# A decoder layer with a state-space mixer on one core: the first block's opening reordered, and the second block's softplus spread over more places

## The reference, cut to what matters

```python
x = x + mixer(layernorm(x))                      # x: 32 sequences of 64 tokens, 512 wide
x = x + attention(layernorm(x), ctx, ctx, mask)
x = x + lora_experts(layernorm(x))

def mixer(h):                                    # 128 heads of 64, 8 groups, state 128
    gate, xBC, dt = split(h @ in_proj_w.T)
    xBC = silu(conv4(xBC) + conv_b)              # causal, 4 taps
    hs, B, C = split(xBC)
    dt = softplus(dt + dt_bias)
    cum = cumsum(dt * -exp(A_log))               # along the tokens
    y = (C @ B.T * exp(cum_i - cum_j) * dt) @ hs + D * hs    # causal
    g = y * silu(gate)
    return rms_norm_by_group(g) * norm_w @ out_w.T
```

## Time and profile before

| | |
|---|---|
| median of 3 runs | 2931.94 us |
| the profiled execution, its own time | 2934.74 us |
| its span | 2932.8 us |
| TensorE busy | 97% of the span |
| VectorE, ScalarE, GpSimd busy | 69%, 50%, 44% |
| mean granted TensorE clock | 0.983 |
| chain that ended last | TensorE 86%, VectorE 8%, ScalarE 3% |

### The profile page before, as it was taken

The page is one execution under the profiler, slowest core; times in us unless marked ns, Lnnn a source line. Parts: engine busy times, 40 slices in busy tenths (PEclk is TensorE's granted clock), DMA queues, the critical chain, the costliest instruction groups (busy, mean ns, idle before and its releaser), DMA issues.

```text
span 2932.8 us, 56348 instructions
## 1 busy us (share of the span) xinstructions
PE 2842.4 (97%) x22240; PEld 2295.3 (78%) x22240; DVE 2022.1 (69%) x3160; ACT 1453.3 (50%) x2184; POOL 1305.0 (44%) x834
## 2 busy tenths in 40 slices
PE   4999999999999999999999999999999999999997
PEld 3777787777878888887888878888888888888875
DVE  6677777777666766677666676677666666666657
ACT  3655665555453555544444544554545454454433
POOL 3576666566443334434334433334334334343423
PEclk8999999999999999999999999999999999999996
DMA  6778777777655655656656655555655555565520
GB/s 190 263 265 280 272 260 255 249 262 237 218 187 184 194 171 185 194 173 187 203 182 197 195 170 184 182 182 186 200 182 187 192 188 185 181 196 177 180 94 19
DMA packets 179267, 578.26 MB, mean 197 GB/s; under 512 B 25216, under 2 KB 31872, under 8 KB 170816
## 3 DMA queue, kind: packets, MB, share of 16 engines
q1 hardware_dynamic: 179008, 574.66, 59.7%
HBM read 460.29 MB, written 114.29 MB: 196 GB/s over the span
## 4 chain that ended last, share of the span: by engine, by line
PE 86%; DVE 8%; ACT 3%; issue 2%; DMA 0%; POOL 0%; DVEq 0%; ACTq 0%; SPq 0%; POOLq 0%
PE p_in L433 49%; PE p_out L433 22%; PE p_y L433 9%; PE p_in L512 4%; DVE cv L1199 2%; DVE t_y L1235 1%; PE p_y L618 1%; ACT cv L809 1%; ACT L809 1%; DVE decay L1212 1%; DVE o_ring L1143 1%; DVE cum L1163 0%; ACT w_ring L809 0%; ACT g_sq L809 0%; DVE g_f L1247 0%
## 5 line engine op out<-in xcount | busy, mean ns | idle before, releaser
L433 PE MATMUL p_in<-xnb,w_ring 128*128 128x512 f32 x6912 | 1702.5, 399 | 22.6 <-DVE cv L1199 17.9
L433 PEld LDWEIGHTS p_in<-xnb,w_ring 128*128 128x128 f32 x6912 | 1276.3, 189 | 294.9 <-issue 22.3
L1199 DVE SCALAR_TENSOR_TENSOR cv<-p_in,cpar,cv 128x504 f32<-128x504 f32 (+2 forms) x960 | 704.5, 734 | 478.1 <-ACT cv L809 454.2
L1551 POOL TENSOR_TENSOR g_lo<-g_f,g_hi 128x512 fp32r<-128x512 f32 x256 | 340.9, 1331 | 1299.3 <-ACT g_hi L809 1299.3
L433 PE MATMUL p_out<-o_ring,g_hi 128*128 128x512 f32 x2048 | 640.3, 394 | 0.0
L809 ACT ACTIVATE cv<-p_in,cpar 128x512 f32<-128x512 f32 x320 | 248.2, 776 | 681.8 <-PE p_in L433 605.5
L433 PEld LDWEIGHTS p_out<-o_ring,g_hi 128*128 128x128 f32 x2048 | 380.9, 188 | 80.9
L433 PE MATMUL p_out<-o_ring,g_lo 128*128 128x512 f32 x1024 | 400.6, 391 | 0.0
L1223 DVE TENSOR_TENSOR x_tok<-p_in,dts 128x512 f32<-128x512 f32 x256 | 176.7, 690 | 299.9 <-PE p_in L512 298.5
L809 ACT ACTIVATE x_t<-cv 128x512 f32<-128x512 f32 x256 | 160.9, 629 | 324.4 <-DVE t_y L1235 295.0
L1562 POOL TENSOR_TENSOR ss<-ss,g_sq 128x512 f32<-128x512 f32 x190 | 304.8, 1604 | 7.5
(11 more groups left out here) (237 smaller groups left out, 2264.5 us busy)
## 6 DMA issues: line engine op xcount, KB each, us to landing
w_ring<-ws_scr SPq DMA_DIRECT2D x432, 512.0 KB, 3.7
o_ring<-ows_scr SPq DMA_DIRECT2D x192, 512.0 KB, 4.6
ws_scr<-w_ring SPq DMA_DIRECT2D x144, 512.0 KB, 5.0
decay<-cum_scr SPq DMA_DIRECT2D x128, 512.0 KB, 6.6
raw_w<-wt SPq DMA_DIRECT2D x144, 256.0 KB, 4.2
ows_scr<-o_ring SPq DMA_DIRECT2D x64, 512.0 KB, 6.1
raw_o<-owt SPq DMA_DIRECT2D x64, 256.5 KB, 5.4
acb<-x SPq DMA_DIRECT2D x3, 1024.0 KB, 8.0
```

Source lines behind the costliest of these rows:

```text
L433: return nc.tensor.matmul(o, lhsT=l, rhs=r, start=first, stop=last)
L1199: ins = V.scalar_tensor_tensor(acc[:, :, t:SEQ], src[:, :, 0:SEQ - t], cpar[:, 5 * m + 3 - t:5 * m + 4 - t], acc[:, :, t:SEQ], ALU.mult, A ...
L1551: T(g_lo[:, c % 2, :], g_f[:, c % 2, :], g_hi[:, c % 2, :].bitcast(F32), ALU.subtract).then_inc(glo_done, 1)
```

## The change

It has these parts, all in the first pass or ahead of it, except where it is said:

- Opening. SP loads the four x tiles first, then the step weights and the identity. VectorE takes the statistics of all four tiles (`aggregate`), POOL one power over four columns, then VectorE normalises all four into four buffers (`first_tiles`), then takes the four remainders. `step_sizes` is reordered so that 8 of its 12 matmuls need only the rounded halves. ScalarE splits three weight units before `raw_steps`.
- First group. `by_token(0)` stands before units 2 and 3. ScalarE takes the second tap-0 and the refill ahead of the SiLU table. SP loads the second decay block only when the first has landed. POOL's second difference stands one step later, VectorE's clamp of the first block before `x_tokens(1)` and that of the second at step 2.
- In all passes, `normal` of the next block's tile stands at the end of step 2, not at the start of step 3.
- First pass, ScalarE: `square(0)` and `square(1)` go from step 2 to step 3, before the gate; the splits of step 2 (units 12 and 13) go behind the slot and the output weights of step 3. POOL: `g_low(1)` before `sum_squares(1)`.
- First pass: the softplus of block 1, cut into 19 parts, stands at 14 places of groups 4 to 6 (`spread`), most of them between `x_tokens` and `o_low`. The later passes keep their places, with new part numbers.

```diff
@@ sync @@
-            load_x(0)
+            for q in range(QT):
+                load_x(q)
+            sp.dma_start(d_s[:, :], wdt).then_inc(wd_in, 16)
             sp.dma_start(id_sb[:, :], ident).then_inc(const_in, 16)
-            load_x(1)
-            sp.dma_start(d_s[:, :], wdt).then_inc(wd_in, 16)
-            for q in range(2, QT):
-                load_x(q)
...
                 for step in range(-1, CPG):
+                    if first(n) and step == 0:
+                        sp.wait_ge(e_in[0], 32)
+                        load_decay(tb, g, 1)
...
-            for blk in range(2):
-                load_decay(0, 0, blk)
+            load_decay(0, 0, 0)
@@ tensor @@
-                pe.wait_ge(xl_done, QT * (b + 1))
                 j = 0
-                for w, a in ((0, 0), (0, 1), (1, 0)):
+                for w, a in ((0, 0), (1, 0), (0, 1)):
+                    if a == 1:
+                        pe.wait_ge(xl_done, QT * (b + 1))
+                    elif w == 0:
+                        pe.wait_ge(xh_done, QT * (b + 1))
...
-                unit(2, tb, g, n)
-                unit(3, tb, g, n)
                 if not begun:
                     pe.wait_ge(dtr_done, 1)
                     by_token(0)
+                unit(2, tb, g, n)
+                unit(3, tb, g, n)
@@ scalar @@
-            act.wait_ge(const_in, 16 * 4)
-            act.wait_ge(wdl_done, 1)
-            raw_steps(0)
-            exp_steps(0)
-            copy(nega[:, 0:1], als[:, :], ACT.Exp).then_inc(nega_done, 1)
...
-            for k in range(RING_W):
+            for k in range(FIRST_SPLITS):
+                split_w(0, k)
+            act.wait_ge(const_in, 16 * 4)
+            act.wait_ge(wdl_done, 1)
+            raw_steps(0)
+            exp_steps(0)
+            copy(nega[:, 0:1], als[:, :], ACT.Exp).then_inc(nega_done, 1)
+            for k in range(FIRST_SPLITS, RING_W):
                 split_w(0, k)
...
                 tap0(0, n)
+                if not begun:
+                    tap0(1, n)
+                    refill(-1)
                 silu_table()
+                if not begun:
+                    tokens_out(0)
                 silu(0, n)
...
+                    if k == 3 and tb == 0:
+                        square(0, n)
+                        square(1, n)
                     if k % 2 == 0:
                         silu(2 + k, n)
                         gate(k, n)
                         g_high(k - 2, n)
-                        square(k - 2, n)
-                        square(k - 1, n)
+                        if k > 2 or tb >= 1:
+                            square(k - 2, n)
+                            square(k - 1, n)
                         g_high(k - 1, n)
...
-                    refill(k)
-                    slot(k, tb, g)
                     if k == 1 and not begun:
                         exp(0, n)
+                    if k == 3 and tb == 0:
+                        slot(k, tb, g)
+                        refill_o(3)
+                        refill_w(2)
+                        refill_w(3)
+                    elif k == 2 and tb == 0:
+                        refill_o(k)
+                        slot(k, tb, g)
+                    else:
+                        refill(k)
+                        slot(k, tb, g)
@@ vector @@
+            for q in range(QT):
+                dve.wait_ge(x0_in[q], 16)
+                V.bn_stats(st6[:, q, :], acb[:, 0, q, :]).then_inc(ln_own, 1)
+                if q >= 1:
+                    aggregate(q - 1, 2 * q)
+            aggregate(QT - 1, 2 * QT - 1)
+            dve.wait_ge(ln_own, 2 * QT)
+            V.tensor_scalar(ve[:, :], mv[:, :, 1], 1e-5, None, ALU.add).then_inc(var_done, QT)
             dve.wait_ge(wdh_done, 1)
             V.tensor_tensor(wd[:, 1, :, :].rearrange("p k c -> p (k c)"), d_s[:, :],
...
             for q in range(QT):
-                dve.wait_ge(x0_in[q], 16)
-                moments(q, acb[:, 0, q, :])
-                if q >= 1:
-                    lows(q - 1)
-                normal(q, (t_y[:, 0, :], xt[:, :])[q % 2], acb[:, 0, q, :], q - 1 if q >= 2 else None)
-            lows(QT - 1)
+                normal(q, first_tiles[q], acb[:, 0, q, :], None)
+            for q in range(QT):
+                lows(q)
...
+            def spread(k, tb, g):
+
+                if tb == 0 and is_at(tb, g, 4) and k in (4, 6, 7):
+                    softplus(1, {4: (0,), 6: (1,), 7: (2,)}[k])
+                if tb == 0 and is_at(tb, g, 5) and k in (0, 2, 3, 4, 6, 7):
+                    softplus(1, {0: (3,), 2: (4, 5), 3: (6,), 4: (7, 8), 6: (9,), 7: (10, 11, 12)}[k])
+                if tb == 0 and is_at(tb, g, 6) and k in (0, 2, 3, 4, 6):
+                    softplus(1, {0: (13,), 2: (14, 15), 3: (16,), 4: (17,), 6: (18,)}[k])
...
                 late(0, tb, g)
+                spread(0, tb, g)
                 refill_o(0)
...
+                    if k == 1 and not begun:
+                        clamped(0, n)
                     early(k, tb, g)
                     if k == 3:
                         decayed(1, n)
                     x_tokens(k, n)
+                    if k == 1 and not begun:
+                        decayed(0, n)
+                    if k > 3:
+                        spread(k, tb, g)
                     if k != 3:
                         refill_o(k)
-                    if k == 1:
-                        if not begun:
-                            clamped(0, n)
-                            decayed(0, n)
+                    if k == (1 if begun else 2):
                         clamped(1, n)
                     if k == 2 and begun:
                         accumulate(*back)
                     late(k, tb, g)
+                    if k in (2, 3):
+                        spread(k, tb, g)
@@ gpsimd @@
-            for q in range(QT):
-                deviation(q)
+            pool.wait_ge(var_done, QT)
+            T(rstd[:, :], ve[:, :], half_neg[:, :], ALU.pow).then_inc(rstd_done, QT)
...
-                        if not begun:
-                            differences(tb, g, 0, n)
-                        differences(tb, g, 1, n)
+                        differences(tb, g, 1 if begun else 0, n)
...
                     refill(k - 1)
+                    if k == 2 and not begun:
+                        differences(tb, g, 1, n)
...
                         g_low(k - 2, n)
+                        if k == 2 and tb == 0:
+                            g_low(1, n)
```

88 lines of the change are left out of this document (51 added, 37 removed).

## The result

The changed kernel takes **2907.49 us** (median of 6 runs, 2903.53 to 2909.30), the kernel before 2931.93 in the same session (6 runs, 2930.68 to 2932.94). The ratio is 0.9913, with a 95% interval of 0.9902 to 0.9924. The kernel is 24.4 us faster; the forecast was 2900, with a range of 2887 to 2914. So the direction and the range held, and 7.5 us less were gained than the sum said.

What follows compares the result with a forecast made beforehand. PE, busy 97% of the span, bounds the kernel, so only waits and low clock can give time. 9.0 + 6.8 + 3.7 + 20.7 - 8.1 = 32.1 us gained: 2900 us, range 2887 to 2914.

Steps and rivals of the forecast that it cites:

- A: Opening: step size product and softplus start earlier, unit 2 at 43.2 instead of 52.19; 9.0 us gained.
- B: Rest of the first group: shorter PE waits, less time at the lower clock; 6.8 us gained.
- D: Groups six to eight: softplus of block 1 spread over more places; 20.7 us gained.
- C: Groups two to four: next tile's normalisation one step earlier removes a PE wait of 1.23 per group; 3.7 us gained.
- lasts its 5.46: Opening, Part A: the step size product starts at 15.05, not 21.97, and keeps its duration of 5.46 us.
- E: First pass: ScalarE's reorder delays output weight 4's load through POOL and SP's queue; 8.1 us lost.
- the opening is a shift only: Rival, first group waits for something else: B lost, PE waits 3 more, gain 22, 2910 us; chance 0.06.
- I cost all of that at nothing: After the first pass PE hardly waits and later softplus places stay, covered by PE's work: no gain or loss.
- The rival of stalls: DVE's softplus stalls beside POOL eat half of D, 10 us: 2910 us; chance 0.13.
- 0.8 in seven groups: Part E: ScalarE's stall of 2.4 leaves PE idle 0.8 us per group before step 5's transposes, 5.6 in sum.
- E hidden: Rival: idle time on ACT and DVE hides the delay, all but 1 us of E goes, 2893 us; chance 0.27.
- The slower case: First pass: PE waits over 5 us per group for output weight 4; at 6.5 us, 2944 us; chance 0.04.

Runs made afterwards that it cites:

- rerun: The changed kernel once more with no edit: 2908.24 us (2900.49 to 2911.35).
- the experiment on SyncE's order: The changed kernel with SyncE handling the output weights' store and raw load ahead of units 14 and 15 in first-pass step 3: 2898.77 us.
- the opening's own run: The kernel before with only the opening and the first group's reorder: 2916.05 us.
- the parameters early: The 2896.92 us kernel with the group parameters' copy of step 7 ahead of the output weight's refill: 2890.45 us.
- both orders: The changed kernel with SyncE's output weights ahead of units 14 and 15, and the fifth group's ScalarE slot of step 3 behind its splits: 2896.92 us.
- C and E alone: The kernel before with only the moved steps on ScalarE, POOL's order and `normal` one step earlier: 2944.31 us.

## Why the prediction was right, and where it was not

Sorted by what the experiments can part, the forecast of 32.1 was 15.8 for the opening and the first group (A, B), 17.1 for the spread (D without the 3.6 that it took from C's move on ACT) and -0.8 for the moved steps (3.7 + 3.6 - 8.1). Measured alone they gave 15.9, 17.5 and -12.4, in sum 21.0, and together 24.4. (0.9 of the 15.8 need the moved `normal`, so the fair figures are 14.9 and 0.1.) The first two parts were forecast within about a microsecond, and what is missing is in the third: within the whole change it comes to 24.4 - 15.9 - 17.5 = -9.0.

**A and B, 15.8 predicted, 15.9 measured alone.** The sum was right and its parts were not. Unit 2 starts at 39.68 where 43.2 was predicted, 12.5 gained and not 9.0. The term that was mis-sized is the product's "lasts its 5.46": all of that row was at the lower clock, 0.455 us a matmul against 0.25. With the transposes of four tiles in a row ahead of it the recorded clock was full from 13.8, and the product took 3.02, in another execution 4.70 (row and rerun above); that is 2.4 or 0.8 us. The chain from the exponential to the copy of the group parameters was 19.1 us and is 16.2: 2.9 shorter where 2.3 stood, since no stall at all is left in it. The first table copy is at 36.17, not 39.6. In exchange B gave less: from unit 2 to the second group 83.7 us became 80.0, which is 3.7 gained and not 6.8. In the experiment on SyncE's order, without part E's wait of 1.96 us and the clock behind it, the same stretch takes 76.1 (7.6 gained). Two of B's terms were also added a little short: the waits, 8.7 less 1.8, 2.0 and 1.1, are 3.8 and not 3.6, and half of the clock's 3.6 is 1.8 and not 1.6. PE's waits were predicted at 1.8, 2.0 and 1.1:

```profile
56.30 0.63 PE L518 MATMUL p_in<-id_sb,x_t 128*128 128x128 f32 x4 [1.25 <-ACT x_t L815]
61.90 1.16 PE L436 MATMUL p_y<-decay,x_tok 64*64 64x64 f32 x64 [2.20 <-DVE decay L1264]
67.75 0.63 PE L518 MATMUL p_in<-id_sb,x_t 128*128 128x128 f32 x4 [1.73 <-ACT sg L815]
78.15 0.66 PE L518 MATMUL p_in<-id_sb,x_t 128*128 128x128 f32 x4 [1.08 <-ACT x_t L815]
99.00 1.05 PE L518 MATMUL p_in<-id_sb,x_t 128*128 128x128 f32 x4 [1.96 <-ACT x_t L815]
```

The wait of 3.29 is 1.25, the one of 4.00 is 2.20, and one of 1.73 that was not foreseen stands between them and the transposes of the fourth pair. "At most 2 us" is missed by 0.2. The rival that the opening is a shift only is refuted by the opening's own run: it would have lost B and 3 us more.

**C, 3.7 predicted in groups two to four, nothing measured there.** The sign that was named, no PE wait ended by the next block's tile, came true, and the gain did not. The step on ACT held: against the group's start the activation ends 46.0 us in before (181.94) and 44.5 in the changed kernel (164.16), and PE does not wait for it. The step that failed is "Together 3 x 1.23", which takes it that nothing further holds PE. With `normal` alone, 1.17 of the 1.23 stand again behind it; with the moves on ACT and SyncE's order mended, a wait of up to 0.95 at the third unit takes their place; with the parameters early too, one of 0.87 to 0.90 for the gate's activation. The three groups take 251.9 to 253.1 us in every kernel that has no delayed transfer; why about 1 us of waiting per group comes back each time was not found. The other failed step is "I cost all of that at nothing" of the later passes: they gained 2.7 us in every kernel with the moved `normal`, and none in those without. The small waits for the tile and its remainder there had nothing behind them. That C in all, 2.0 in the median alone and 2.9 in the stages, is not far from the 3.7 is luck: it lies where nothing was predicted.

**D, 20.7 predicted (17.1 without C's share), 17.5 alone and 16.2 within.** The mechanism was right: three groups at full clock, and no wait of PE over 1 us in them in the kernel with SyncE's order (with the change as it is, part E's 1.31 and 1.99 are left). What is missing is the 1.2 a group, 3.6 in sum, that "Part C's move on ACT removes here too": the spread alone takes 255.2 us in these groups and keeps waits of 1.4 to 1.5 before the transposes of step 3; with the moves on ACT and both orders those are gone, but waits of up to 0.95 at the third unit have come or grown, and the groups take 254.7, only 0.5 less. The stalls beside POOL: the polynomial's line in these groups, three rows of the chain, and the row of POOL that stands beside the first of them.

```profile
L1206 DVE SCALAR_TENSOR_TENSOR cum<-cum,d_e x7: 680/848/1672, 510.5 to 550.9; 128x512 f32<-128x512 f32 x7
```
```profile
483.61 1.71 DVE L1200 TENSOR_TENSOR d_s<-d_e,cum 128x512 f32<-128x512 f32 x1
...
520.64 3.04 DVE L1206 SCALAR_TENSOR_TENSOR cum<-cum,d_e 128x512 f32<-128x512 f32 x2
549.50 2.13 DVE L1206 SCALAR_TENSOR_TENSOR cum<-cum,d_e 128x512 f32<-128x512 f32 x3
...
483.47 1.30 POOL L1612 TENSOR_TENSOR g_lo<-g_f,g_hi 128x512 fp32r<-128x512 f32 x1
```

The seven operations take 7.1 us, 1.02 each, against 8.5 and 1.21 at the old places: there are stalls, up to 1.71, and fewer than before. The Trainium skill, SBUF — State Buffer, section Who interferes with whom, states that a DVE instruction with two SBUF inputs contends with a GpSimd instruction that reads SBUF. The trace agrees: the operation of 1.71 ran beside POOL's, and the square at 504.08, with POOL idle, took 0.68. Of the 6 us that stalls might have taken from D nothing is seen. The rival of stalls, 2910, is near the measured median by luck: its mechanism is not what held the time.

**E, 8.1 predicted, 11.3 measured within the change and 15.4 alone.** The path was right link by link: four subtractions in a row, the load of the output weight behind the traffic, ACT's wait in step 4, PE's before the transposes of step 5. Put on the old trace's time (this group starts 16.22 us earlier now), the load was foreseen at 190.5, landing near 196.5 (with the row's 6.7 it would be 197.2); it was issued at 191.9, and ACT went on at 196.4. That the landing fits is luck: the issue was 1.4 later than foreseen, and the load landed 4.4 us after it. ACT's stall was 3.05 in the place of 2.4. The term that was mis-sized is "0.8 in seven groups": PE's waits before those transposes are 1.96, 2.32, 2.32, 1.13, 0.71, 1.31, 1.99 and 0.45, 12.2, with 1.77 in the fifth group's step 4. In the second group the activation ended 1.9 later than before, which with the slack of 1.1 would have left the 0.8 of the prediction. But PE came to its transposes 1.5 earlier than in the kernel before, as C intends, and so waited 2.32. One gain cannot be booked in C and its lateness be used as slack in E. The prediction's own sign, a wait over 2 us and so more time, was met in two groups. Then the clock: a wait of 2.3 us was followed by the lower level in one execution and not in another; the window shown has 3.4 us of it, which costs 1.7 us of work. SyncE's order gives back 9.5 where the seven groups were put at 5.6; with the fifth group's stall mended too (1.9, predicted 2.5) E comes to 11.3 within the change, and to 15.4 without A, B and D.

The rival "E hidden" is refuted (21.8 us of waits on ACT). The slower case had the right place and did not reach its point: it needs 5 us of PE's waiting per group, and the longest such wait was 2.56, in the rerun. Yet C and E alone did make the kernel 12.4 us slower, with no A, B and D to outweigh them.

The 7.5 us that are missing, by steps: C's 3.7 and the 3.6 counted in D on its strength were not there, E was 3.2 more, and the later passes gave 2.7 that were not counted: 7.3 + 3.2 - 2.7 = 7.8. So the forecast held its range although one gain was absent and one cost was too small; the two large terms carried it.

## What to carry to other kernels

When a split or a refill is moved later on one engine, follow the DMA queue that is fed by it to its end: here two weight splits moved by one step, with two more behind the output weights, put an unrelated load 4 us later on SyncE, and one reorder of SyncE gave back 9.5 us in a change worth 24. Slack read in a profile belongs to the timing of that profile: if another part of the same change brings the waiting engine earlier, the slack is gone by as much. And a wait removed from a steady loop is worth its length only when the next releaser is earlier too; look at the row behind it, and take the loop's period, not the wait, as the measure.

## What was not expected of the hardware

The same wait has two prices: after 2.31 us of idle PE the granted clock fell to 0.50 in one execution, and after 2.32 us at the same place it stayed at 1.00 in another. In the opening too: the same 12 matmuls took 3.02 or 3.03 in the profiles of four kernels and 4.70 to 4.94 in those of four others with the same opening, as the clock rose before them or within them (first recorded at full at 13.2 to 14.7 us in the first four, at 18.3 to 19.2 in the others). One profile can differ from another by up to 1.9 us for that alone.
